# Masked graph attention on one core: the exchanged products move one step later, the squares come early, and each exchange row becomes one run

## The chip, the cores and the metric

The kernel runs on one core of a Trainium2 chip. The metric is the device time of a whole run in microseconds. A core has TensorE (matrix products; in the profile PE, its weight loads PEld), VectorE (DVE), ScalarE (ACT), GpSimd (POOL) and SyncE (SP), which here only issues transfers. Each engine works through its own queue in order. Semaphores order the engines among one another.

## The reference, cut to what matters

```python
# M = N = 6144, D = 128, TEMPERATURE = 0.07
h = jnp.maximum(_layernorm(x), 0.0)
scores = jnp.where(adj > 0, jnp.einsum('md,de,ne->mn', h, weight, nodes), -2**32 + 1)
out = x + jax.nn.softmax(scores / TEMPERATURE, axis=1) @ nodes
```

`adj` is int32, 6144 x 6144, with about one entry in 1,500 set. It is 151 MB, and all of it has to be read.

## The kernel before

The output is made in 48 tiles of 128 rows. For one tile `u` there are these stages, all of which run over its 6144 columns:

- **h**: layer norm of x (statistics on VectorE, `make_h` on GpSimd), split into two fp16 halves (`split_h`), and turned by a transposing DMA (`hT`).
- **scores**: TensorE, six chunks of 1024 columns, six matmuls each, into the two PSUM tiles `ps_s`. Chunk j can start when chunk j-2 has been masked.
- **mask**: VectorE (L603), six chunks: score less code, and the row's maximum. The codes are the adjacency, which is loaded in three chunks of 2048 columns (`load_adj`, 1 MB each, SyncE) and turned into codes by GpSimd (`convert`, L425). The buffer `adj_i` holds one tile, so chunk c of the next tile is loaded when both masks over chunk c are done. `find_max` (L611, L613) ends the row's maximum.
- **exp**: ScalarE, one piece of 2048 columns (`exp_p`, L491) and four pieces of 1024 (`exp_e`, L497).
- **turning**: the products need the probabilities transposed. The first 2048 columns are turned on TensorE (`turn`, L813, four turns of 512 columns into the three PSUM banks `ps_t`) and split into fp16 halves by ScalarE (`hi_p`, L522) and VectorE (`lo_p`, L618). The other 4096 columns are turned as 32 x 32 squares on VectorE (`turn_squares`, L630, four pieces) and then exchanged between the four groups of 32 partitions by 16 SBUF to SBUF transfers of 128 KB (`exchange`, L338, SyncE). ScalarE (`hi_e`, L505, four pieces) and GpSimd (`lo_e`, L444, eight turns) split them.
- **product**: TensorE adds twelve turns into `ps_o`: `product_p` 0 to 3 for the turned ones, `product_e` 0 to 7 for the exchanged ones. `finish` (VectorE) scales and adds x, and ScalarE stores.

The tiles are worked on in a pipeline written out by hand. In step t, scores and masks belong to tile t+2, exp and squares to tile t+1, turns and products to tile t (`product_e` 4 to 7 to tile t-1), and `make_h` to tile t+3. Steps 3 to 38 are a hardware loop of six iterations with six steps in each; the steps before and after are written out.

The order of SyncE's queue in a step is: adjacency chunk 2 of t+2, x of t+4, adjacency chunk 0 of t+3, the transpose of h, eight exchange transfers of t+1, adjacency chunk 1 of t+3, eight exchange transfers, x for the residual. ScalarE's order is: `exp_e` 0 to 2, `hi_p` 0 and 1, the store, `exp_e` 3, `hi_e` 0, `hi_p` 2 and 3, `hi_e` 1 to 3, `exp_p`. VectorE's is: mask 0, square 0, mask 1, `finish`, square 1, `lo_p` 0 and 1, mask 2, square 2, `lo_p` 2 and 3, mask 3, square 3, mask 4, the sum, statistics, mask 5, `find_max`. GpSimd's is: `lo_e` 6 and 7 of t-1, convert chunk 1, `make_h`, `split_h`, convert chunk 2, `lo_e` 0 to 5, convert chunk 0.

`hi_e` waits for all 16 transfers of its tile:

```python
act.wait_ge(exchanged[s], exchanges(u, s))
```

Of the kernel before, what the change touches and what calls it, by code (L numbers as in the profile page):

```python
# [5 lines left out]
def gnn_masked_attention_kernel(  # L6
# [71 lines left out]
    EARLY_E = 4  # L78
# [19 lines left out]
    with ctx:  # L98
# [15 lines left out]
        pT_hi = sb("pT_hi", [P, BANKS, TURN], fp16)  # L114
        pT_lo = sb("pT_lo", [P, BANKS, TURN], fp16)
# [3 lines left out]
        h_centred = sb("h_centred", [P, 2, D], fp32)  # L119
# [4 lines left out]
        fin_a = sb("fin_a", [P, 2, D], fp32)  # L124
# [15 lines left out]
        nodes_max = sb("nodes_max", [P, 1], fp32)  # L140
        nodes_top = sb("nodes_top", [P, 1], fp32)
# [6 lines left out]
        w_sum = sb("w_sum", [P, 1], fp32)  # L148
        w_top = sb("w_top", [P, 1], fp32)
        y_bound = sb("y_bound", [P, 1], fp32)  # L150
# [112 lines left out]
        def exchanged_part(r, c):  # L263


            return probs[:, r, columns(E_FIRST + E_PART * c, E_PART)].rearrange("q (a k i) -> q a k i", a=QUADS, i=QUAD)
# [36 lines left out]
        def _(sp):  # L303
# [54 lines left out]

# [20 lines left out]
        def _(pool):  # L379
# [7 lines left out]
            def make_h(u, s):  # L387
                pool.wait_ge(aggr_done, u + 1)
# [8 lines left out]
                nc.gpsimd.tensor_scalar(h_centred[:, s, :], x_ln[:, s, :], mean_var[:, s, 0:1], 0.0,  # L397
# [6 lines left out]
                nc.gpsimd.tensor_scalar(h[:, s, :], h_centred[:, s, :], rstd[:, s, :], 1.0, ALU.mult, ALU.mult)\  # L404
# [72 lines left out]
            for m in range(E_TURNS - E_PART, E_TURNS):  # L477
# [3 lines left out]
        def _(act):  # L481
# [478 lines left out]
```

## Time and profile before

| | |
|---|---|
| median of 3 runs | 1142.36 us (1138.94 to 1143.82) |
| profiled execution | 1133.46 us, span 1131.7 us |
| mean granted clock of TensorE | 0.97 |
| TensorE busy (modelled) | 82% of the span |
| GpSimd busy | 75% |
| VectorE busy | 70% |
| ScalarE busy | 58% |
| SyncE's DMA queue | 264 MB, 82% of 16 engines |

The span runs from the first to the last instruction of the profiled execution. Busy shares are means over a span whose stages overlap; idle time of an engine matters only where it delays the work that sets the end. Matmuls are pipelined and their ends are modelled, so the busy time of TensorE counts overlaps. The releaser behind an idle time is inferred from semaphores. An instruction row of the timeline gives its start, its length, engine, line, operation, output and input; "x2" means that two have been merged.

### The profile page before, as it was taken

Reading aid. Unit: us, or ns where it says so; the run is one execution under the profiler, and the core shown is the slowest. Engines: PE = TensorE matmul, PEld = TensorE weight load, DVE = VectorE, ACT = ScalarE, POOL = GpSimd, SP = SyncE. Lnnn points to the kernel's source line nnn. Section 1 sums busy time; section 2 is a strip of 40 time slices with the busy share of each in tenths; the row PEclk is TensorE's granted clock in tenths of the full one; section 3 lists DMA queues with packets and bytes.
Section 4 is the critical chain, followed back from the end, with each engine's and each line's share of the span. In section 5 each row is a group of like instructions: output and inputs, shape, how many; then the busy total and the mean of one; then the engine's idle time right before and its main releaser. Section 6 shows DMA issues by size and latency. Waiting matters only on the chain.

```text
span 1131.7 us, 23242 instructions
## 1 busy us (share of the span) xinstructions
PE 930.1 (82%) x7182; PEld 614.6 (54%) x7182; DVE 790.5 (70%) x1430; ACT 652.5 (58%) x896; POOL 844.2 (75%) x825
## 2 busy tenths in 40 slices
PE   7688888879788797896978878888789888888876
PEld 4255555556555465563655545555556555555555
DVE  6777677767676676775776657767676776777672
ACT  5466555655565555654565545646565665656563
POOL 4967887786778767787678776778678778878755
PEclk9999999999999998999999989999999999999999
DMA  9489889887988879889788887889978988998873
GB/s 317 150 212 280 225 250 265 250 246 213 246 270 228 250 208 269 237 255 240 200 267 232 253 254 202 238 235 262 267 211 242 266 275 228 260 282 228 221 185 83
DMA packets 171522, 268.81 MB, mean 238 GB/s; under 512 B 29968, under 2 KB 152976, under 8 KB 152976
## 3 DMA queue, kind: packets, MB, share of 16 engines
q1 hardware_dynamic: 164208, 264.05, 82.0%
q10 hardware_dynamic: 7200, 3.28, 1.4%
q8 instruction: 67, 1.10, 0.4%
q14 instruction: 47, 0.39, 0.1%
HBM read 160.50 MB, written 3.15 MB: 145 GB/s over the span
## 4 chain that ended last, share of the span: by engine, by line
SPq 24%; PE 16%; issue 14%; DMA 13%; DVE 12%; POOL 8%; ACT 7%; ACTq 1%; DVEq 1%; POOLq 0%
SPq L338 22%; PE ps_s L795 7%; POOL nodes_raw L444 7%; DMA probs<-nodes_raw 5%; PE ps_o L822 5%; DMA probs<-squares_own 5%; ACT pT_e_hi L505 4%; DVE probs L603 4%; DMA adj_i<-in_adj_dram 3%; ACT pT_hi L522 3%; DVE pT_lo L618 2%; PE ps_o L825 2%; DVE nodes_raw L630 2%; DVE squares_own L630 2%; PE ps_t L813 2%
## 5 line engine op out<-in xcount | busy, mean ns | idle before, releaser
L603 DVE CUSTOM_DVE_ANT_0 probs<-ps_s,adj_i 128x1024 f32<-128x1024 f32 x282 | 343.0, 1217 | 242.3 <-POOL adj_i L425 104.0
L444 POOL TENSOR_TENSOR nodes_raw<-probs,pT_e_hi 128x512 f16<-128x512 f32 x384 | 433.4, 1163 | 19.6 <-ACT pT_e_hi L505 19.6
L795 PE MATMUL ps_s<-yT_hi,hT 128*128 128x512 f16 x1152 | 402.0, 391 | 36.5 <-issue 26.2
L425 POOL TENSOR_SCALAR adj_i<-adj_i 128x2048 uint32<-128x2048 int32 x141 | 268.6, 1905 | 214.5 <-DMA adj_i<-in_adj_dram 208.9
L497 ACT ACTIVATE probs<-probs,neg_max,exp_scale 128x1024 f32<-128x1024 f32 x192 | 237.1, 1236 | 197.3 <-DVE neg_max L613 191.2
L822 PE MATMUL ps_o<-v,pT_e_hi 128*128 128x256 f16 x1536 | 287.8, 277 | 50.2 <-POOL nodes_raw L444 47.2
L825 PE MATMUL ps_o<-v,nodes_raw 128*128 128x128 f16 x1536 | 271.6, 221 | 0.0
L505 ACT ACTIVATE pT_e_hi<-probs 128x1024 f16<-128x1024 f32 x192 | 192.4, 1057 | 113.7 <-DMA probs<-squares_own 65.3
L822 PE MATMUL ps_o<-v,pT_hi 128*128 128x256 f16 x768 | 145.5, 283 | 103.8 <-DVE pT_lo L618 103.7
L795 PE MATMUL ps_s<-yT_lo,hT 128*128 128x512 f16 x576 | 225.7, 392 | 0.0
L822 PEld LDWEIGHTS ps_o<-v,pT_e_hi 128*128 128x128 f16 x1536 | 151.8, 99 | 129.1 <-POOL nodes_raw L444 98.6
L795 PEld LDWEIGHTS ps_s<-yT_hi,hT 128*128 128x128 f16 x1152 | 115.5, 100 | 155.5 <-issue 48.1
L522 ACT ACTIVATE pT_hi<-ps_t 128x512 f16<-128x512 f32 x192 | 103.5, 591 | 134.9 <-PE ps_t L813 134.8
L822 PEld LDWEIGHTS ps_o<-v,pT_hi 128*128 128x128 f16 x768 | 77.2, 101 | 158.1 <-DVE pT_lo L618 132.6
L825 PEld LDWEIGHTS ps_o<-v,nodes_raw 128*128 128x128 f16 x1536 | 152.0, 99 | 15.3 <-issue 2.2
L618 DVE TENSOR_TENSOR pT_lo<-ps_t,pT_hi 128x512 f16<-128x512 f32 x192 | 121.7, 674 | 47.6 <-ACT pT_hi L522 47.6
L825 PE MATMUL ps_o<-v,pT_lo 128*128 128x128 f16 x768 | 139.5, 226 | 0.0
L630 DVE STREAM_TRANSPOSE nodes_raw<-probs 128x1024 f32<-128x1024 f32 x96 | 119.0, 1239 | 1.4 <-ACT probs L497 1.4
L630 DVE STREAM_TRANSPOSE squares_own<-probs 128x1024 f32<-128x1024 f32 x96 | 119.0, 1239 | 0.5 <-ACT probs L497 0.5
L491 ACT ACTIVATE probs<-probs,neg_max,exp_scale 128x2048 f32<-128x2048 f32 x48 | 100.4, 2092 | 8.6 <-DVE neg_max L613 8.6
L813 PE MATMUL ps_t<-ident,probs 128*128 128x128 f32 x768 | 100.3, 274 | 0.0
L813 PEld LDWEIGHTS ps_t<-ident,probs 128*128 128x128 f32 x768 | 82.7, 141 | 1.5 <-issue 0.3
(72 smaller groups left out, 537.8 us busy)
## 6 DMA issues: line engine op xcount, KB each, us to landing
adj_i<-in_adj_dram SPq DMA_DIRECT2D x141, 1024.0 KB, 6.5
probs<-squares_own SPq DMA_DIRECT2D x384, 128.0 KB, 3.1
probs<-nodes_raw SPq DMA_DIRECT2D x384, 128.0 KB, 3.6
nodes_raw<-in_L_gnn_input_dram SPq DMA_DIRECT2D x6, 512.0 KB, 7.0
x_res<-in_x_dram SPq DMA_DIRECT2D x48, 64.0 KB, 4.5
probs<-in_adj_dram SPq DMA_DIRECT2D x3, 1024.0 KB, 14.1
out_dram<-fin ACTq DMA_DIRECT2D x48, 64.0 KB, 4.8
x_ln<-in_x_dram SPq DMA_DIRECT2D x46, 64.0 KB, 5.8
```

What stands on the lines that cost most here:

```text
L338: sp.dma_start(to.rearrange("j (c a x) -> j c a x", a=QUADS, c=E_PARTS)[:, :, a, :], squares[s][a * QUAD:(a + 1) * QUAD, b, :, :].rearrang ...
L425: nc.gpsimd.tensor_scalar(codes(u, c), adjacency(u, c), PRESENT_STEP, ABSENT, ALU.mult, ALU.add)\
L444: nc.gpsimd.tensor_tensor(lo, exchanged_part(r, c)[:, :, g * PER_TURN:(g + 1) * PER_TURN, :], hi, ALU.subtract)\
L497: nc.scalar.activation(part, part, ACT.Exp, bias=neg_max[:, s, :], scale=exp_scale[:, :], accum_out=chunk_sum[:, s, 1 + c:2 + c]).then_inc ...
L505: nc.scalar.activation(e_halves(pT_e[0], E_PART * c, E_PART), exchanged_part(r, c), ACT.Copy)\
L603: nc.vector.tensor_tensor_reduce(out=probs[:, r, j * SCORE:(j + 1) * SCORE], in0=ps_s[j % 2][:, :], in1=codes(u, c)[:, part * SCORE:(part ...
L618: nc.vector.tensor_tensor(pT_lo[:, P_BANK[q], :], ps_t[P_BANK[q]][:, :], pT_hi[:, P_BANK[q], :], ALU.subtract)\
L630: nc.vector.transpose(squares[s][:, :, c * blocks:(c + 1) * blocks, :], of).then_inc(squared, 1)
L795: made = nc.tensor.matmul(ps_s[j % 2][:, q * 512:(q + 1) * 512], hT[:, s, part, :], y[:, cols], start=(part == 0 and y is yT_hi), stop=(pa ...
L813: made = nc.tensor.transpose(ps_t[P_BANK[q]][:, b * P:(b + 1) * P], probs[:, r, q * TURN + b * P:q * TURN + (b + 1) * P], ident[:, :])
L822: nc.tensor.matmul(ps_o[:, 0:2 * D], hi[b], v[:, blk, :, :].rearrange("p s d -> p (s d)"), start=(order == 0 and b == 0), stop=(order == T ...
L825: made = nc.tensor.matmul(ps_o[:, 0:D], lo[b], v[:, blk, 0, :], start=False, stop=(order == TURNS - 1 and b == PER_TURN - 1), skip_group_c ...
```

## The change

- TensorE takes all eight `product_e` of tile t-1 in step t, between the score chunks 0 to 3; then `product_p` 0 and 1 after chunk 4 and 2 and 3 after chunk 5.
- `pT_hi` and `pT_lo` have four buffers of one turn each, where there were three. `hi_p` waits for the product of the step before from its own buffer alone.
- ScalarE does all four `exp_e`, then `hi_p` 0 and 1, four `hi_e`, `hi_p` 2 and 3, the store and `exp_p`.
- VectorE does the squares 1 to 3 right after mask 1, and `finish` after mask 3.
- In the exchange, a piece of a row lies in one run of 4 KB in source and target, where there were four runs of 1 KB. The exchanged pieces of a turn are therefore spread over all 4096 columns, and masks 2 to 5 of a tile wait for all eight `lo_e` of the tile that was in the buffer.
- GpSimd does three `lo_e` of t-1, then `make_h` and `split_h`, convert chunk 1, three `lo_e`, convert chunk 2, two `lo_e`, convert chunk 0.
- `h_centred` has one buffer (`make_h` waits for `h_done`), `fin_a` is gone (`finish` writes `fin` twice), and some scalars share one tensor.
- SyncE's order stays.

```diff
-    EARLY_E = 4
+    LATE_LO = 3
...
-        pT_hi = sb("pT_hi", [P, BANKS, TURN], fp16)
-        pT_lo = sb("pT_lo", [P, BANKS, TURN], fp16)
+        pT_hi = sb("pT_hi", [P, P_TURNS, TURN], fp16)
+        pT_lo = sb("pT_lo", [P, P_TURNS, TURN], fp16)
...
-            return probs[:, r, columns(E_FIRST + E_PART * c, E_PART)].rearrange("q (a k i) -> q a k i", a=QUADS, i=QUAD)
+            all_of_it = probs[:, r, columns(E_FIRST, E_TURNS)].rearrange("q (a k i) -> q a k i", a=QUADS, i=QUAD)
+            return all_of_it[:, :, E_PART * PER_TURN * c:E_PART * PER_TURN * (c + 1), :]
...
-                        sp.dma_start(to.rearrange("j (c a x) -> j c a x", a=QUADS, c=E_PARTS)[:, :, a, :],
-                                     squares[s][a * QUAD:(a + 1) * QUAD, b, :, :].rearrange("j (c k) i -> j c (k i)", c=E_PARTS))\
+                        sp.dma_start(to.rearrange("j (a x) -> j a x", a=QUADS)[:, a, :],
+                                     squares[s][a * QUAD:(a + 1) * QUAD, b, :, :].rearrange("j k i -> j (k i)"))\
...
             def make_h(u, s):
+                if not (isinstance(u, int) and u == 0):
+                    pool.wait_ge(h_done, u)
...
                 if at != 0:
-                    for m in range(E_TURNS - E_PART, E_TURNS):
+                    for m in range(E_TURNS - LATE_LO, E_TURNS):
                         lo_e(t - 1, (r - 1) % PROBS, m)
-                if has(at, 2):
-                    convert(t + 2, 1)
                 if has(at, 3):
                     make_h(t + 3, 1 - par)
                     split_h(t + 3, 1 - par)
                 if has(at, 2):
+                    convert(t + 2, 1)
+                for m in range(0, 3):
+                    lo_e(t, r, m)
+                if has(at, 2):
                     convert(t + 2, 2)
-                for m in range(E_TURNS - E_PART):
+                for m in range(3, E_TURNS - LATE_LO):
                     lo_e(t, r, m)
...
             def hi_p(t, q, at):
                 act.wait_ge(turned, t * P_TURNS + (q + 1))
-                if P_BANK.index(P_BANK[q]) != q:
-
-                    act.wait_ge(pv_done, t * TURNS + (P_BANK.index(P_BANK[q]) + 1))
-                elif at != 0:
-                    act.wait_ge(pv_done, t * TURNS + (max(k for k in range(P_TURNS) if P_BANK[k] == P_BANK[q]) + 1 - TURNS))
-                nc.scalar.activation(pT_hi[:, P_BANK[q], :], ps_t[P_BANK[q]][:, :], ACT.Copy).then_inc(hi_done, 1)
+                if at != 0:
+
+                    act.wait_ge(pv_done, t * TURNS + (q + 1 - TURNS))
+                nc.scalar.activation(pT_hi[:, q, :], ps_t[P_BANK[q]][:, :], ACT.Copy).then_inc(hi_done, 1)
...
                 if has(at, 1):
-                    for c in range(3):
+                    for c in range(E_PARTS):
                         exp_e(t + 1, nxt, n, c)
                 for q in range(2):
+                    hi_p(t, q, at)
+                for c in range(E_PARTS):
+                    hi_e(t, par, r, c, at)
+                for q in range(2, P_TURNS):
                     hi_p(t, q, at)
...
-                if has(at, 1):
-                    exp_e(t + 1, nxt, n, 3)
-                hi_e(t, par, r, 0, at)
-                for q in range(2, P_TURNS):
-                    hi_p(t, q, at)
-                for c in range(1, E_PARTS):
-                    hi_e(t, par, r, c, at)
...
-                    dve.wait_ge(lo_e_done, (u - PROBS) * E_TURNS + E_PART * (j - 1))
+                    dve.wait_ge(lo_e_done, (u - PROBS) * E_TURNS + E_TURNS)
...
                 next_mask(0)
                 next_squares(0)
                 next_mask(1)
+                for c in range(1, E_PARTS):
+                    next_squares(c)
+                next_mask(2)
+                lo_p(t, 0)
+                lo_p(t, 1)
+                next_mask(3)
                 if at != 0:
                     finish(t - 1, nxt, at is None or at > 2)
-                next_squares(1)
-                lo_p(t, 0)
-                lo_p(t, 1)
-                next_mask(2)
-                next_squares(2)
                 lo_p(t, 2)
                 lo_p(t, 3)
-                next_mask(3)
-                next_squares(3)
                 next_mask(4)
...
-                for j in range(2):
-                    scores(t, par, j, at)
+                def last_products(m, turns):
                     if at != 0:
-                        for m in range(EARLY_E + 2 * j, EARLY_E + 2 * j + 2):
-                            product_e(t - 1, m, None if at is None else at - 1)
-                for j in range(2, 4):
-                    for q in range(2 * j - 4, 2 * j - 2):
-                        turn(t, r, q, at)
-                    scores(t, par, j, at)
-                    if j == 2 and at != 0:
-                        pe.wait_ge(fin_done, t)
-                    for q in range(2 * j - 4, 2 * j - 2):
-                        product_p(t, q, at)
-                for j in range(4, SCORES):
-                    scores(t, par, j, at)
-                    for m in range(2 * j - 8, 2 * j - 6):
-                        product_e(t, m, at)
+                        for k in range(m, m + turns):
+                            product_e(t - 1, k, None if at is None else at - 1)
+
+                scores(t, par, 0, at)
+                last_products(0, 2)
+                scores(t, par, 1, at)
+                last_products(2, 2)
+                for q in range(2):
+                    turn(t, r, q, at)
+                scores(t, par, 2, at)
+                last_products(4, 2)
+                scores(t, par, 3, at)
+                last_products(6, 2)
+                for q in range(2, P_TURNS):
+                    turn(t, r, q, at)
+                scores(t, par, 4, at)
+                if at != 0:
+                    pe.wait_ge(fin_done, t)
+                for q in range(2):
+                    product_p(t, q, at)
+                scores(t, par, 5, at)
+                for q in range(2, P_TURNS):
+                    product_p(t, q, at)
```

## Rows read from the trace of the kernel before

**Rows 1.** The page: busy time of the engines, and the queue of SyncE.

```profile
PE 930.1 (82%) x7182; PEld 614.6 (54%) x7182; DVE 790.5 (70%) x1430; ACT 652.5 (58%) x896; POOL 844.2 (75%) x825
...
q1 hardware_dynamic: 164208, 264.05, 82.0%
```

**Rows 2.** Line 611, which ends a step: its 48 instructions, first and last.

```profile
L611 DVE TENSOR_REDUCE row_max<-chunk_max x48: 158/159/160, 42.0 to 1093.7; 128x1 f32<-128x6 f32 x48
```

**Rows 3.** Six steps in one window: busy us, clock, DMA share, GB/s.

```profile
core 0: us, PE busy (x) PEld busy (x) DVE busy (x) ACT busy (x) POOL busy (x), PEclk, DMA share, GB/s
874.40:1004.20 129.80, 110.96 (x890) 73.41 (x888) 96.12 (x174) 78.96 (x108) 103.48 (x103) 1.00 0.90 256
```

**Rows 4.** Waits of those six steps: total us, times, longest.

```profile
ACT probs L497 <- DVE neg_max L613: 25.1, 6, 4.4
...
POOL adj_i L425 <- DMA adj_i<-in_adj_dram: 15.6, 9, 2.8
DVE probs L603 <- POOL adj_i L425: 15.4, 7, 2.6
```

**Rows 5.** Timeline of ScalarE, then of VectorE, around one landing.

```profile
925.44 1.24 ACT L497 ACTIVATE probs<-probs,neg_max,exp_scale 128x1024 f32<-128x1024 f32 x1
...
928.62 1.06 ACT L505 ACTIVATE pT_e_hi<-probs 128x1024 f16<-128x1024 f32 x1 [1.84 <-DMA probs<-squares_own]
929.59 1.07 ACT L522 ACTIVATE pT_hi<-ps_t 128x512 f16<-128x512 f32 x2
930.54 2.96 ACT L505 ACTIVATE pT_e_hi<-probs 128x1024 f16<-128x1024 f32 x3
933.38 2.10 ACT L491 ACTIVATE probs<-probs,neg_max,exp_scale 128x2048 f32<-128x2048 f32 x1
...
930.20 1.29 DVE L618 TENSOR_TENSOR pT_lo<-ps_t,pT_hi 128x512 f16<-128x512 f32 x2 [0.68 <-ACT pT_hi L522]
931.40 1.22 DVE L603 CUSTOM_DVE_ANT_0 probs<-ps_s,adj_i 128x1024 f32<-128x1024 f32 x1
932.54 1.24 DVE L630 STREAM_TRANSPOSE nodes_raw<-probs 128x1024 f32<-128x1024 f32 x1
```

**Rows 6.** Timeline of SyncE's queue: exchange issues.

```profile
912.54 5.16 SPq L338 DMA_DIRECT2D probs<-squares_own  x8
...
918.39 5.97 SPq L338 DMA_DIRECT2D probs<-squares_own  x8
...
933.87 5.18 SPq L338 DMA_DIRECT2D probs<-nodes_raw  x8
```

**Rows 7.** Timeline of TensorE where the loop goes back.

```profile
528.93 0.39 PE L795 MATMUL ps_s<-yT_hi,hT 128*128 128x512 f16 x1 [2.99 <-issue]
...
535.88 0.61 PE L795 MATMUL ps_s<-yT_hi,hT 128*128 128x512 f16 x1 [4.17 <-issue]
```

**Rows 8.** Timeline of GpSimd in one step.

```profile
926.05 0.19 POOL L390 TENSOR_SCALAR var_eps<-mean_var 128x1 f32<-128x1 f32 x1
...
929.08 0.43 POOL L416 TENSOR_TENSOR h_split<-h,h_split 128x128 f16<-128x128 f32 x1
931.37 1.93 POOL L425 TENSOR_SCALAR adj_i<-adj_i 128x2048 uint32<-128x2048 int32 x1 [1.86 <-DMA adj_i<-in_adj_dram]
933.26 6.76 POOL L444 TENSOR_TENSOR nodes_raw<-probs,pT_e_hi 128x512 f16<-128x512 f32 x6
```

**Rows 9.** Issues of lines 338 and 309: ns min/median/max.

```profile
L338 SPq DMA_DIRECT2D probs<-squares_own x384: 585/607/1932, 54.1 to 1098.0; - x192
...
L309 SPq DMA_DIRECT2D adj_i<-in_adj_dram x141: 327/365/1927, 10.4 to 1079.3; - x141
```

**Rows 10.** Windows: exchange alone, exchange with a backlog, adjacency.

```profile
1107.00:1116.00 9.00, 6.90 (x72) 5.52 (x70) 1.90 (x4) 2.35 (x4) 4.21 (x4) 1.00 0.90 207
...
923.00:926.00 3.00, 2.76 (x22) 1.74 (x19) 2.96 (x7) 1.65 (x3) 1.91 (x1) 1.00 1.13 229
927.00:932.00 5.00, 4.39 (x42) 3.28 (x40) 4.32 (x7) 3.38 (x5) 2.46 (x5) 1.00 1.06 404
```

**Rows 11.** Timeline of VectorE near the end.

```profile
1104.10 1.24 DVE L630 STREAM_TRANSPOSE nodes_raw<-probs 128x1024 f32<-128x1024 f32 x1
```

More of the change, by code:

```diff
@@ L118, in gnn_masked_attention_kernel @@
         hT = sb("hT", [P, 2, 2, P], fp16)
-        h_centred = sb("h_centred", [P, 2, D], fp32)
+        h_centred = sb("h_centred", [P, D], fp32)
         h = sb("h", [P, 2, D], fp32)
@@ L123, in gnn_masked_attention_kernel @@
         x_res = sb("x_res", [P, 2, D], fp32)
-        fin_a = sb("fin_a", [P, 2, D], fp32)
         fin = sb("fin", [P, 2, D], fp32)
@@ L139, in gnn_masked_attention_kernel @@
         part_max = sb("part_max", [P, NODE_PARTS], fp32)
-        nodes_max = sb("nodes_max", [P, 1], fp32)
-        nodes_top = sb("nodes_top", [P, 1], fp32)
+        head_scalars = sb("head_scalars", [P, 5], fp32)
+        nodes_max, nodes_top, w_sum, w_top, y_bound = [head_scalars[:, i:i + 1] for i in range(5)]
         field = sb("field", [P, 1], int32)
@@ L396, in make_h @@
                 pool.sem_inc(pool_waited, 1)
-                nc.gpsimd.tensor_scalar(h_centred[:, s, :], x_ln[:, s, :], mean_var[:, s, 0:1], 0.0,
+                nc.gpsimd.tensor_scalar(h_centred[:, :], x_ln[:, s, :], mean_var[:, s, 0:1], 0.0,
                                         ALU.subtract, ALU.max).then_inc(h_centred_done, 1)
@@ L403, in make_h @@
                 pool.sem_inc(pool_waited, 1)
-                nc.gpsimd.tensor_scalar(h[:, s, :], h_centred[:, s, :], rstd[:, s, :], 1.0, ALU.mult, ALU.mult)\
+                nc.gpsimd.tensor_scalar(h[:, s, :], h_centred[:, :], rstd[:, s, :], 1.0, ALU.mult, ALU.mult)\
                     .then_inc(h_done, 1)
@@ L476, in _ @@
             steps(pool, step)
-            for m in range(E_TURNS - E_PART, E_TURNS):
+            for m in range(E_TURNS - LATE_LO, E_TURNS):
                 lo_e(LAST, LAST % PROBS, m)
@@ L617, in lo_p @@
                 dve.wait_ge(hi_done, split_count(t, q))
-                nc.vector.tensor_tensor(pT_lo[:, P_BANK[q], :], ps_t[P_BANK[q]][:, :], pT_hi[:, P_BANK[q], :], ALU.subtract)\
+                nc.vector.tensor_tensor(pT_lo[:, q, :], ps_t[P_BANK[q]][:, :], pT_hi[:, q, :], ALU.subtract)\
                     .then_inc(split_freed, 1)
@@ L644, in finish @@
                 dve.wait_ge(x_res_in[s], loads(u, s))
+                if free:
+                    dve.wait_ge(stored[s], loads(u - 2, s))
                 dve.wait_ge(pv_done, u * TURNS + TURNS)
-                nc.vector.scalar_tensor_tensor(out=fin_a[:, s, :], in0=ps_o[:, 0:D], scalar=inv_sum[:, s, :],
+                nc.vector.scalar_tensor_tensor(out=fin[:, s, :], in0=ps_o[:, 0:D], scalar=inv_sum[:, s, :],
                                                in1=x_res[:, s, :], op0=ALU.mult, op1=ALU.add)\
@@ L649, in finish @@
                 dve.wait_ge(fin_a_done, u + 1)
-                if free:
-                    dve.wait_ge(stored[s], loads(u - 2, s))
                 nc.vector.scalar_tensor_tensor(out=fin[:, s, :], in0=ps_o[:, D:2 * D], scalar=inv_sum[:, s, :],
-                                               in1=fin_a[:, s, :], op0=ALU.mult, op1=ALU.add)\
+                                               in1=fin[:, s, :], op0=ALU.mult, op1=ALU.add)\
                     .then_inc(fin_done, 1)
@@ L831, in product_p @@
                 pe.wait_ge(split_freed, split_count(t, q))
-                multiply(q, [pT_hi[:, P_BANK[q], b * P:(b + 1) * P] for b in range(PER_TURN)],
-                         [pT_lo[:, P_BANK[q], b * P:(b + 1) * P] for b in range(PER_TURN)], q, at)
+                multiply(q, [pT_hi[:, q, b * P:(b + 1) * P] for b in range(PER_TURN)],
+                         [pT_lo[:, q, b * P:(b + 1) * P] for b in range(PER_TURN)], q, at)
             def product_e(t, m, at):
@@ L915, in step @@
             def step(t, par, r, at):
[L916 to L917 removed]
+                def last_products(m, turns):
                     if at != 0:
[L919 to L932 removed]
+                        for k in range(m, m + turns):
[20 more added lines that the diff above has]
+                    product_p(t, q, at)
             steps(pe, step)
[L935 removed]
+            for m in range(E_TURNS):
                 product_e(LAST, m, LAST)
```

4 lines of the change are left out of this document (removed).

## Prediction, made before the change was run

> **What bounds the kernel now.** I began with the page's busy line and queue line [rows 1]. No engine is near full: TensorE 82%, GpSimd 75%, VectorE 70%, ScalarE 58%; but the 16 DMA engines spend 82% of the span on SyncE's queue. A bound is then either the DMA stream or a loop through several queues. The mark of a step is `find_max`: 48 of them lie between 42.0 and 1093.7 us [rows 2], so a step takes 22.4 us on average. For a stretch without disturbance I took the six steps from 874.4 to 1004.2 us: 21.6 us each, with VectorE busy 16.0, ScalarE 13.2, GpSimd 17.2, TensorE 18.5 (modelled) and the DMA share 0.90, so 19.5 us of DMA [rows 3]. Two to five microseconds of every step belong to no engine. The waits of that stretch say where: ScalarE for the maximum, GpSimd for adjacency landings, VectorE for GpSimd's codes [rows 4]. These point round in a circle, so I followed one event in the timeline. ScalarE starts `hi_e` 0 at 928.62, the moment the exchange has landed; behind it on the same in-order engine stand `hi_p` 2 and 3 (929.59); then VectorE does `lo_p` 2 and 3 (930.20), mask 3 (931.40) and square 3 (932.54), and only now may SyncE start the next exchange, at 933.87 [rows 5]. That is 5.25 us from landing to issue. The exchange before it was issued from 912.54 and had landed at 928.62: 16.1 us. 5.25 + 16.1 = 21.3 us is the step. The 16.1 are 8 issues in 5.2, an adjacency issue between, 8 more issues in 6.0 [rows 6], and the rest landing behind the 1 MB of adjacency in the same queue. So the bound is a one-step loop: an exchange cannot begin until the exchange before it has landed, because the last square stands behind work that waits for that landing.
>
> A second loss comes every six steps, when the loop goes back: TensorE waits for "issue" twice, 2.99 and 4.17 us [rows 7]. It and other irregularities are the 0.75 us by which the mean step (22.4) exceeds the quiet one.
>
> **The change part by part.**
>
> *Squares early.* All four squares of t+1 now stand behind masks 0 and 1 alone. ScalarE does the four `exp_e` first. Let T be the start of mask 0. Masks take 1.15 to 1.2 us from start to start, squares 1.16 (932.54 less 931.40 is 1.14) [rows 5], so two masks and four squares end near T+7.2; `exp_e` 3 is done about T+4.6, since `exp_e` starts before mask 0. No work is added, it is the same 16.0 us of VectorE. The loop of rows 5 is cut: squares no longer wait for `lo_p` 2 and 3.
>
> *Products one step later.* TensorE takes the eight exchanged products of t-1 in step t, between scores 0 to 3. `hi_e`(t) moves behind four `exp_e` and `hi_p` 0 and 1. An exchange whose squares end at T+7.2 lands, by the 16.1 us above, at T+23.3. With a step P of 19.2 this is 4.1 us into the next step; `hi_e` comes up there at about 6 us (four `exp_e` at 1.24, two `hi_p` at 0.54 [rows 5]). Slack about 2 us, so the wait for the landing goes. What is late next is the loop over two steps: landing, four `hi_e`, two `hi_p`, `exp_p`, four `exp_e`, a square, an exchange: 3.9 + 1.1 + 2.1 + 4.9 + 1.2 + 16.1 = 29.3 us for two steps, 14.7 for one. It does not bind.
>
> *Waits added.* Masks 2 to 5 wait for all eight `lo_e` of t-1. GpSimd does its last three first in its step, 3.4 us, and mask 2 stands at T+7.2: covered. Without that cover lo_p, masks and finish queue behind it and TensorE waits for them. The wait on `h_done` names GpSimd's own earlier result: nothing. Convert 1 moves behind `make_h` and `split_h`: three `lo_e` 3.4, `make_h` and split 3.5 (926.05 to 929.51), convert 1.9: it ends at T+8.8, and mask 2 waits up to 1.6 us for it; masks 3 to 5 queue behind. TensorE has eight products, two score chunks and turns in that time, so scores 4 is where it shows. I leave 1.6 of VectorE per step: 16.0 + 1.6 + about 0.6 of handshakes = 18.2.
>
> *Four half buffers, one `fin`, one `h_centred`.* `hi_p` 3 no longer waits for product 0 of its tile; bank 0 of `ps_t` is still shared, so turn 3 still waits for `lo_p` 0. The second `finish` operation reads the row the first wrote, as before. Nothing either way; the operations are of the same shape.
>
> *Adjacency and queue order.* SyncE issues the same 16 exchange DMAs, three adjacency loads, two x loads and a transpose in the same order. The adjacency load amid the exchange waits for mask 3, which now comes after the squares (about T+11.5); the first 8 issues run until about T+13, so it is covered, and if issues get cheaper the DMA queue has a backlog to live on.
>
> *The exchange's shape.* Each row of an exchange DMA is now one run of 4 KB instead of four of 1 KB. The trace shows no such transfer. Issue costs 0.61 us at four runs a row, and at best 0.33, the shortest adjacency issue [rows 9]; I take 0.5, and it is off the path once the transfers themselves are the slower. The transfer: with nothing else moving, the exchange shows 0.90 share at 207 GB/s, so 230 GB/s at full share; with a backlog 229; adjacency moves at 404 [rows 10]. If 4 KB runs go as 1 KB runs, 16 take 2.1 MB / 229 = 9.2 us; if they reach the adjacency's rate, 5.2. A bad end is not excluded: each of the 16 engines gets two runs in place of eight, less to overlap. I take twice the time as a worst case, 18.3. Nearest is the same source, target and engines, so I take 9.2, hardly changed.
>
> The rate alone fits the row above. The Trainium skill, "DMA: Bandwidth & Descriptors", section "Why small descriptors are slow (HBM only)", holds that SBUF to SBUF transfers don't suffer from small descriptors, and puts the fixed price at about 3 cycles on each packet's 32-byte beats. As an estimate from that page, 35 beats for 1 KB against 131 for 4 KB is 6% less, so the exchange would be 8.6 us in place of 9.2. No row of the trace before can show it.
>
> **The new step.** GpSimd: eight `lo_e` at 1.12 (six in 6.76), three converts at 1.9, `make_h` and split 3.5 [rows 8] = 18.2. DMA: 9.2 + 3.15 MB / 404 = 7.8, + 1 to 1.5 for x, the output and the transpose = 18.0 to 18.5, and at the share of now at most 19.5. TensorE at most 18.5, VectorE 18.2. Four resources within half a microsecond: the floor is 18.3, and they won't all fit without gaps. I take 19.2, between the floor and 19.5 of DMA with a few tenths of gaps. The gain is 21.6 - 19.2 = 2.4 us on 46 steps, 110 us. The 0.75 us of irregularity I keep: TensorE has no room to catch up 7 us.
>
> The tail: the last square starts at 1104.10 and ends at 1105.3 now [rows 11], behind turns and low halves; with `exp_e` of the last tile from 1094.1 they would end about 1100.3. The exchange, the eight `lo_e` and the products then follow as before: about 4 us. In the start the products come later and the scores do not: nothing.
>
> Span 1131.7 - 110 - 4 = 1018. The profiled execution took 1133.46, 1.8 more than its span, so 1020; the median of the runs, 1142.36, is 0.8% above the profiled one, so **1028 us**.
>
> **The rivals.** A: the 4 KB runs are cheap. At 5.2 us an exchange the DMA stream falls to 14.5 and only the compute floors are left; a step of 18.4, another 0.8 x 46 = 37 us: 990. For it: adjacency, in 8 KB runs, goes at 404. Against: the exchange at 230 with nothing beside it, where packets have no rival to wait for.
>
> B: the gaps. GpSimd and VectorE wait for each other twice a step (convert to mask, `lo_e` to product to `finish`), and a full DMA queue lands adjacency late; if the 15.6 us of waits for it in six steps [rows 4] stay, they and GpSimd's 18.2 make 20.8, with a little overlap 20.5: 1028 + 1.3 x 46 = 1088.
>
> C: nothing gained. The exchange was never the only reason: the step is 21 to 22 because the DMA stream (19.5 us by its share) with its pauses is. 1120 to 1150. Against it: the 5.25 us of [rows 5], in which the next exchange waits for nothing but the last square.
>
> D, slower: the 4 KB runs are slow. `hi_e` blocks ScalarE in order, with `hi_p` 2 and 3 and `exp_p` behind it. With the rest of DMA at 9.1 us, the step exceeds today's 21.6 once an exchange DMA takes over 0.78 us against 0.57 now. At twice the time the step is 18.3 + 9.1 = 27.4 us: 1142 + 5.8 x 46 = 1409, and at 0.9 us each 23.5: 1230.
>
> **Numbers.** Forecast 52% (1000 to 1055), A 18%, B 20%, C 4%, D 6%. The range leaves out C and D, and a quarter of A and of B, whose own spreads reach past the ends: 985 to 1095. A change of 0.5% is about what a measurement of this kernel can tell. Faster 0.91, same 0.02, slower 0.07.
>
> **What would show it.** Right: `hi_e` no longer waits for exchanged data; the last square to the first exchange issue lies near T+7; steps near 19.2; DMA share 0.93 or more; GpSimd above 90% within a step. The exchange alone near 207 to 230 GB/s says the shape did nothing, near 400 says A. Wrong: steps over 20.5 with waits of VectorE for `adj_i`, or of ScalarE for landings. The forecast falls if a wait I count as covered (mask 2 for convert 1, TensorE for `finish`, SyncE for mask 3) grows beyond 2 us.

## The result and the profile after

The changed kernel takes 1008.35 us (median of 4 runs, 1006.03 to 1012.51) beside 1142.01 us for the kernel before; the ratio is 0.884, 95% interval 0.880 to 0.887. Predicted were 1028 us in a range of 985 to 1095. The same kernel run again beside three experiments gave 1009.19 us and 0.887 (0.880 to 0.894). The kernel before varied between groups of runs (medians 1131 to 1142), so experiments are compared by their ratio to the kernel before on the same chip.

The page of the changed kernel, first the busy line and SyncE's queue, then line 606, which ends a step as 611 did:

```profile
PE 890.9 (88%) x7182; PEld 618.5 (61%) x7182; DVE 791.6 (79%) x1430; ACT 646.6 (64%) x896; POOL 842.6 (84%) x825
...
q1 hardware_dynamic: 90480, 264.05, 95.6%
```

```profile
L606 DVE TENSOR_REDUCE row_max<-chunk_max x48: 158/159/160, 39.8 to 972.5; 128x1 f32<-128x6 f32 x48
```

VectorE, ScalarE and GpSimd are busy as long as in [rows 1] to within 1%, and TensorE does the same 7182 matmuls (its modelled busy time is 39 us less); the same work lies in a shorter span, and the DMA queue has gone from 82 to 95.6%. The span fell by 1131.7 - 1007.0 = 124.7 us. Of these, 2.2 lie ahead of the first mark (42.0 against 39.8) and 3.5 behind the last (38.0 against 34.5); 119.0 are steps: 47 of them took 1051.7 us [rows 2] and take 932.7. A step fell from 22.4 to 19.85 us. Six quiet ones, in the view of [rows 3]:

```profile
857.40:972.50 115.10, 107.07 (x901) 75.89 (x899) 95.74 (x170) 77.78 (x108) 100.00 (x97) 1.00 1.03 282
```

That is 19.2 us a step, the number of the forecast (the mean of the 37 steps that remain from the sixth mark on, without the long step of every six, is 19.35), with a DMA share of 1.03 (transfers overlap a little, so it can pass 1) and 282 GB/s against 256. The waits, for the whole span:

```profile
POOL nodes_raw L442 <- ACT pT_e_hi L505: 98.3, 45, 6.9
DVE probs L598 <- POOL adj_i L423: 75.9, 67, 1.9
...
ACT pT_e_hi L505 <- DMA probs<-squares_own: 50.1, 20, 4.2
...
ACT pT_e_hi L505 <- DMA probs<-nodes_raw: 42.8, 18, 4.0
```

Here is the first thing that I had not forecast: `hi_e` still waits for exchanged data, 92.9 us in 38 steps. The timelines of SyncE, ScalarE and GpSimd over one step show why, in the manner of [rows 5, 6]:

```profile
788.77 5.43 SPq L335 DMA_DIRECT2D probs<-nodes_raw  x8
794.47 0.40 SPq L306 DMA_DIRECT2D adj_i<-in_adj_dram  x1
794.92 5.77 SPq L335 DMA_DIRECT2D probs<-nodes_raw  x8
...
788.72 3.90 ACT L505 ACTIVATE pT_e_hi<-probs 128x1024 f16<-128x1024 f32 x4 [2.03 <-DMA probs<-squares_own]
...
807.79 3.90 ACT L505 ACTIVATE pT_e_hi<-probs 128x1024 f16<-128x1024 f32 x4 [2.17 <-DMA probs<-nodes_raw]
...
789.96 3.39 POOL L442 TENSOR_TENSOR nodes_raw<-probs,pT_e_hi 128x512 f16<-128x512 f32 x3 [0.82 <-ACT pT_e_hi L505]
```

The exchange issued from 788.77 has landed at 807.79: 19.0 us, where it took 16.1. SyncE issues as fast as before; the transfers stand in a queue that is now always full. It is not this exchange alone: the median from issue to landing of one transfer, in the kernel before and then in the changed one, is

```profile
probs<-squares_own SPq DMA_DIRECT2D x384, 128.0 KB, 3.1
probs<-nodes_raw SPq DMA_DIRECT2D x384, 128.0 KB, 3.6
```

```profile
probs<-squares_own SPq DMA_DIRECT2D x384, 128.0 KB, 6.6
probs<-nodes_raw SPq DMA_DIRECT2D x384, 128.0 KB, 7.5
```

The chain of waits over two steps names a loop again:

```profile
780.35 3.39 POOL nodes_raw L442 x3
...
787.36 1.21 SPq L359
...
799.34 8.35 DMA probs<-nodes_raw
...
811.26 1.17 POOL nodes_raw L442
...
818.36 2.29 POOL nodes_raw L442 x2
```

From `lo_e` at 780.35 it goes over `make_h`, `split_h` and the transpose of h, behind which the exchange stands in SyncE's queue, to the landing at 807.69, to `hi_e`, and through GpSimd's codes and halves to 818.36: 38.0 us, two steps of 19.0. So the exchange is in a loop still, but in one that spans two steps and has most of GpSimd's work in it. It is not the only loop of this length. From 641.50 to 681.07, 39.6 us, the chain runs from GpSimd over mask 2, `finish`, TensorE's products and `hi_e` back to GpSimd without any landing. The page puts 14% of the chain on the exchange's issues and 10% on its landings, against 22 and 10% before.

### The profile page after: what moved, and what is told of

Read it like the earlier page. It is cut to its first block, busy times and chain, and to the rows that moved or that the text cites. A ratio compares the mean times of both kernels' runs of the same rounds, so it can differ in the third digit from the quotient of the medians.

```text
span 1007.0 us, 23278 instructions
## 1 busy us (share of the span) xinstructions
PE 890.9 (88%) x7182; PEld 618.5 (61%) x7182; DVE 791.6 (79%) x1430; ACT 646.6 (64%) x896; POOL 842.6 (84%) x825
## 3 DMA queue, kind: packets, MB, share of 16 engines
q1 hardware_dynamic: 90480, 264.05, 95.6%
## 4 chain that ended last, share of the span: by engine, by line
PE 24%; POOL 21%; SPq 16%; issue 14%; DMA 10%; DVE 6%; ACT 4%; POOLq 0%; DVEq 0%; ACTq 0%
SPq L335 14%; POOL nodes_raw L442 12%; PE ps_s L789 10%; PE ps_o L816 8%; DMA probs<-nodes_raw 6%; POOL adj_i L423 5%; DMA probs<-squares_own 4%; PE ps_o L819 4%; ACT pT_e_hi L505 3%; DVE probs L598 2%; PE ps_t L807 2%; DVE pT_lo L613 1%; POOL h_centred L395 1%; SPq L359 1%; POOL rstd L391 1%
## 5 line engine op out<-in xcount | busy, mean ns | idle before, releaser
L598 DVE CUSTOM_DVE_ANT_0 probs<-ps_s,adj_i 128x1024 f32<-128x1024 f32 x282 | 343.3, 1218 | 147.9 <-POOL adj_i L423 75.9
L789 PE MATMUL ps_s<-yT_hi,hT 128*128 128x512 f16 x1152 | 396.7, 386 | 45.6 <-issue 29.9
L816 PE MATMUL ps_o<-v,pT_e_hi 128*128 128x256 f16 x1536 | 276.8, 275 | 0.0
L423 POOL TENSOR_SCALAR adj_i<-adj_i 128x2048 uint32<-128x2048 int32 x141 | 268.3, 1903 | 10.2 <-DMA adj_i<-in_adj_dram 10.0
L819 PE MATMUL ps_o<-v,nodes_raw 128*128 128x128 f16 x1536 | 266.3, 220 | 0.0
L505 ACT ACTIVATE pT_e_hi<-probs 128x1024 f16<-128x1024 f32 x192 | 188.4, 1046 | 112.2 <-DMA probs<-squares_own 50.1
L789 PE MATMUL ps_s<-yT_lo,hT 128*128 128x512 f16 x576 | 222.6, 386 | 0.0
L816 PE MATMUL ps_o<-v,pT_hi 128*128 128x256 f16 x768 | 138.6, 274 | 19.2 <-DVE fin L647 14.6
L807 PE MATMUL ps_t<-ident,probs 128*128 128x128 f32 x768 | 108.0, 276 | 40.5 <-DVE pT_lo L613 40.5
L819 PE MATMUL ps_o<-v,pT_lo 128*128 128x128 f16 x768 | 132.7, 220 | 0.0
L625 DVE STREAM_TRANSPOSE nodes_raw<-probs 128x1024 f32<-128x1024 f32 x96 | 113.9, 1223 | 3.1 <-ACT probs L497 1.4
L625 DVE STREAM_TRANSPOSE squares_own<-probs 128x1024 f32<-128x1024 f32 x96 | 113.9, 1223 | 2.3 <-ACT probs L497 0.6
L816 PEld LDWEIGHTS ps_o<-v,pT_hi 128*128 128x128 f16 x768 | 75.5, 98 | 52.4 <-DVE fin L647 33.1
## 6 DMA issues: line engine op xcount, KB each, us to landing
probs<-in_adj_dram SPq DMA_DIRECT2D x3, 1024.0 KB, 14.5
```

The costliest lines, as they stand in the source:

```text
L423: nc.gpsimd.tensor_scalar(codes(u, c), adjacency(u, c), PRESENT_STEP, ABSENT, ALU.mult, ALU.add)\
L505: nc.scalar.activation(e_halves(pT_e[0], E_PART * c, E_PART), exchanged_part(r, c), ACT.Copy)\
L598: nc.vector.tensor_tensor_reduce(out=probs[:, r, j * SCORE:(j + 1) * SCORE], in0=ps_s[j % 2][:, :], in1=codes(u, c)[:, part * SCORE:(part ...
L625: nc.vector.transpose(squares[s][:, :, c * blocks:(c + 1) * blocks, :], of).then_inc(squared, 1)
L789: made = nc.tensor.matmul(ps_s[j % 2][:, q * 512:(q + 1) * 512], hT[:, s, part, :], y[:, cols], start=(part == 0 and y is yT_hi), stop=(pa ...
L807: made = nc.tensor.transpose(ps_t[P_BANK[q]][:, b * P:(b + 1) * P], probs[:, r, q * TURN + b * P:q * TURN + (b + 1) * P], ident[:, :])
```

## The experiments

**1. `hi_p` 2 and 3 ahead of `hi_e` 0, in the kernel before.** It tests the loop that the prediction named as the bound.

```diff
-                hi_e(t, par, r, 0, at)
                 for q in range(2, P_TURNS):
                     hi_p(t, q, at)
-                for c in range(1, E_PARTS):
+                for c in range(E_PARTS):
```

> The kernel before with one edit: ScalarE does hi_p 2 and 3 ahead of hi_e 0. Theory (the 21.3 us step is the one-step loop landing, hi_e 0, hi_p 2 and 3, lo_p, mask 3, square 3, next exchange): the loop is cut, a quiet step falls to 19.5 to 20.5 us and the time to 1035 to 1085 us. Rival (a second loop of nearly the same length stands behind it: landing, hi_e, eight lo_e on GpSimd, the last products, finish, square 1, and the squares behind it, over two steps): the step stays at 21 to 21.6 and the time within 1.5% of 1142 us.

1117.04 us, 0.986 (0.978 to 0.995). That is outside the theory's 1035 to 1085 us and within the rival's 1.5%. The marks of its steps, in VectorE's timeline:

```profile
883.42 0.16 DVE L610 TENSOR_REDUCE row_max<-chunk_max 128x1 f32<-128x6 f32 x1
901.43 0.16 DVE L610 TENSOR_REDUCE row_max<-chunk_max 128x1 f32<-128x6 f32 x1
924.97 0.16 DVE L610 TENSOR_REDUCE row_max<-chunk_max 128x1 f32<-128x6 f32 x1
945.49 0.16 DVE L610 TENSOR_REDUCE row_max<-chunk_max 128x1 f32<-128x6 f32 x1
968.84 0.16 DVE L610 TENSOR_REDUCE row_max<-chunk_max 128x1 f32<-128x6 f32 x1
```

Steps of 18.0, 23.5, 20.5 and 23.4 us: single steps can now be short, but a pair still takes 41.5 and 43.9. The loop of one step was real: the waits of `hi_e` for landings fell from 110.8 to 17.6 us in the whole run. What stands behind it here is not the exchange loop that the rival named, though. Pieces of this kernel's chain, over one step:

```profile
886.61 6.70 DMA adj_i<-in_adj_dram
...
893.51 1.91 POOL adj_i L425
...
902.93 7.05 DMA adj_i<-in_adj_dram
...
910.16 1.91 POOL adj_i L425
...
917.50 1.17 DVE nodes_raw L629
```

The exchange is issued from 897.48, the adjacency chunk stands behind eight of its transfers in SyncE's queue and lands at 909.98, GpSimd makes codes of it, then come masks, `lo_p` 2 and 3, mask 3 and square 3, and the next exchange is issued at 918.75: 21.3 us, one step. This loop goes through an adjacency landing. On the page of this run 9% of the chain are adjacency landings and 1% exchange landings; in the kernel before it was 3% and 10%. In other stretches, as from 949 to 986, the chain goes round over GpSimd's halves, the products, `finish` and `hi_e` without a landing.

In the kernel before there is a loop of two steps as well, of nearly the length of two short ones. It can be followed there: `hi_e` 0 after a landing at 907.29, `lo_e` from 911.83, the last of them done at 922.7, `finish` at 924.15, then the squares behind it, and the exchange from 933.87, landed at 950.85: 43.6 us for two steps.

**2. Squares early alone, in the kernel before.** The products stay where they were.

```diff
-                    for c in range(3):
+                    for c in range(E_PARTS):
                         exp_e(t + 1, nxt, n, c)
...
                 next_mask(1)
+                for c in range(1, E_PARTS):
+                    next_squares(c)
                 if at != 0:
                     finish(t - 1, nxt, at is None or at > 2)
-                next_squares(1)
```

> The kernel before with the squares 1 to 3 right after mask 1 and exp_e 3 with the others, ahead of finish; the products stay in their step, the exchange keeps four runs a row. Theory (early squares are what cuts every loop through the exchange): 1010 to 1060 us, most of the gain. Rival (the products have to move too, since mask 5 and find_max wait behind products that wait for lo_e): 1080 to 1130 us.

1083.4 us, 0.955 (0.949 to 0.962): two fifths of the whole gain, as the rival said, but not for the reason it gave. TensorE and VectorE at one place of a step:

```profile
716.50 0.28 PE L819 MATMUL ps_o<-v,pT_hi 128*128 128x256 f16 x1 [2.61 <-DVE pT_lo L616]
...
711.74 3.49 DVE L628 STREAM_TRANSPOSE nodes_raw<-probs 128x1024 f32<-128x1024 f32 x3
...
715.76 1.28 DVE L616 TENSOR_TENSOR pT_lo<-ps_t,pT_hi 128x512 f16<-128x512 f32 x2
```

TensorE stands still for 2.6 us, because `product_p` 0 comes right after scores 2, and its low half stands behind three squares. Of the 47 steps 19 take 20.22 to 20.24 us and none after the first is shorter. What holds them there is a loop of TensorE and VectorE alone, without the exchange; on the page 56% of the chain are TensorE's and 2% landings. The waits of TensorE's products for `lo_p` are 133.6 us in this run and 4.6 in the changed kernel (there its turns wait 40.5 for `lo_p`). This is what moving the products does: products that need nothing from this step fill the hole that early squares tear into TensorE's step. The changed kernel differs from this one in GpSimd's order, the four half buffers and the order of `lo_p` and `finish` too; these were not tried one by one.

**3. Squares late, in the changed kernel.** The complement: products late, squares 2 and 3 behind `lo_p` 1 and mask 3.

```diff
-                for c in range(1, E_PARTS):
-                    next_squares(c)
+                next_squares(1)
                 next_mask(2)
                 lo_p(t, 0)
                 lo_p(t, 1)
+                next_squares(2)
                 next_mask(3)
+                next_squares(3)
```

> The changed kernel with VectorE's squares late again: square 1 after mask 1, square 2 after lo_p 1, square 3 after mask 3. Theory (the exchange has to start early in the step to land before hi_e needs it): the last square ends some 5 us later, hi_e and GpSimd wait for the landing, a quiet step of 20 to 20.8 us, the time 1045 to 1090 us. Rival (products one step later leave slack enough, squares early are not needed): 1005 to 1020 us.

1084.95 us, 0.956 (0.950 to 0.962), in the theory's range. The steps are longer than its 20 to 20.8, 21.3 us at the mean of the 37 without the sixth ones; the sixth is 22.5 where the changed kernel's is 25.2. The waits:

```profile
ACT probs L497 <- DVE neg_max L608: 156.0, 47, 4.0
POOL nodes_raw L442 <- ACT pT_e_hi L505: 149.4, 48, 7.2
...
PE ps_o L817 <- DVE fin L647: 102.6, 46, 2.8
...
ACT pT_e_hi L505 <- DMA probs<-squares_own: 64.0, 16, 5.0
```

Both waits that the theory names are there (the landing 135 us with the other buffer's, against 92.9 in the changed kernel, GpSimd for `hi_e` 149 against 98), and TensorE waits another 103 for `finish` (14.6 in the changed kernel), since squares 2 and 3 now stand between mask 2, which waits for codes, and `finish`. How much of the loss is the late landing and how much the late `finish` is not taken apart. Early squares alone are worth 4.5%, all the rest of the change without them 4.4%, both together 11.5%.

**4. The shape of the exchange,** in both kernels: 4 KB runs put into the kernel before, and 1 KB runs back into the changed one.

```diff
-                        sp.dma_start(to.rearrange("j (c a x) -> j c a x", a=QUADS, c=E_PARTS)[:, :, a, :],
-                                     squares[s][a * QUAD:(a + 1) * QUAD, b, :, :].rearrange("j (c k) i -> j c (k i)", c=E_PARTS))\
+                        sp.dma_start(to.rearrange("j (a x) -> j a x", a=QUADS)[:, a, :],
+                                     squares[s][a * QUAD:(a + 1) * QUAD, b, :, :].rearrange("j k i -> j (k i)"))\
```

> The kernel before with one run of 4 KB in each row of the exchange, and masks 2 to 5 waiting for all eight lo_e. Theory (the shape does little, the transfer is as slow as with four runs of 1 KB): 1125 to 1150 us. Rival (bigger runs make the exchange faster, and the landing comes earlier in the loop): 1085 to 1120 us.

> The changed kernel with the exchange's four runs of 1 KB a row, all else as changed. Theory (the shape does little): 1000 to 1020 us. Rival (with the DMA queues full, per-run work and 0.1 us more at each issue count): 1025 to 1060 us.

The kernel before with 4 KB: 1129.34 us, 0.997 (0.993 to 1.001), no change. Its packet records give 286 ns for a run of 4 KB at the median; in the kernel before one of 1 KB took 72, and four of them 288. The changed kernel with 1 KB: 1016.02 us, 0.898 (0.891 to 0.904) against 0.884 (0.880 to 0.887) and 0.887 (0.880 to 0.894) of the changed kernel: about 1% slower, but the second interval touches, so it is not settled. The queue is full there, and all exchange packets together took 524 us of the 16 engines against 489, 7% more. In the kernel before it was 438 against 418, 5%. The Trainium skill, "DMA: Bandwidth & Descriptors", section "Why small descriptors are slow (HBM only)", holds that SBUF to SBUF transfers don't suffer from small descriptors; in packet time they do here, by 5 and 7%, near the 6% that the prediction worked out as an estimate from the section's price per packet.

The four sums also part shape and queue. Per step they are 9.1 us (1 KB, queue with pauses), 8.7 (4 KB, with pauses), 10.9 (1 KB, full) and 10.2 (4 KB, full): the longer runs take a little off, and the full queue adds 1.5 us and more.

**5. What bounds the changed kernel.** Three cuts, each of which leaves work out. Half of each exchange transfer left out:

```diff
-                        sp.dma_start(to.rearrange("j (a x) -> j a x", a=QUADS)[:, a, :],
-                                     squares[s][a * QUAD:(a + 1) * QUAD, b, :, :].rearrange("j k i -> j (k i)"))\
+                        sp.dma_start(to.rearrange("j (a x) -> j a x", a=QUADS)[:, a, 0:TURN],
+                                     squares[s][a * QUAD:(a + 1) * QUAD, b, 0:TURN // QUAD, :].rearrange("j k i -> j (k i)"))\
```

> The changed kernel with half of the exchange left out: each of the 16 transfers moves 2 KB of its 4 KB a row, so the output isn't the reference's. DMA work falls by some 4.5 us a step, everything else is as it was. Theory (a quiet step of 19.0 us is set by a loop through the exchange, full DMA queues and GpSimd): the waits of hi_e for landings go and the step falls to GpSimd's 18.2 to 18.4 us, the time to 970 to 985 us. Rival (engines alone set it, the landing waits cost nothing): 1000 to 1012 us.

Half of GpSimd's codes left out:

```diff
-                nc.gpsimd.tensor_scalar(codes(u, c), adjacency(u, c), PRESENT_STEP, ABSENT, ALU.mult, ALU.add)\
+                nc.gpsimd.tensor_scalar(codes(u, c)[:, 0:SCORE], adjacency(u, c)[:, 0:SCORE], PRESENT_STEP, ABSENT, ALU.mult, ALU.add)\
```

> The changed kernel with half of GpSimd's codes left out (each convert takes 1024 of its 2048 columns), so the output isn't the reference's. GpSimd's work falls by 2.9 us a step. Theory (the loop runs through GpSimd as well as through the exchange; DMA share is 1.04, so the stream can't follow far): the step falls by 0.2 to 0.8 us, 970 to 1000 us. Rival (GpSimd alone is the bound): the step falls by 1 us or more to TensorE's 17.7 to 18, 945 to 965 us. Second rival (DMA alone is the bound): no change.

Both:

> Both cuts at once, half of the exchange and half of the codes left out. Theory: with the stream and GpSimd out of the way TensorE and the handshakes between it and VectorE are left, a step of 17.7 to 18.2 us, 940 to 965 us. Rival (the step's order on VectorE and TensorE already binds at 18.5 or more): 975 to 990 us, no better than one cut alone.

And the unedited kernel beside them:

> The changed kernel unedited, so that the three runs beside it and those of the call before have it on their own chip. Expected 0.88 to 0.89 of the kernel before.

| | us | ratio (interval) | mean of the 37 steps, us |
|---|---|---|---|
| changed kernel | 1009.19 | 0.887 (0.880 to 0.894) | 19.35 |
| half the exchange | 958.19 | 0.842 (0.836 to 0.849) | 18.03 |
| half the codes | 997.02 | 0.878 (0.871 to 0.884) | 19.15 |
| both | 923.62 | 0.810 (0.803 to 0.818) | 17.44 |

The half exchange and both together came out below their ranges (970 to 985, 940 to 965), half the codes within its own.

Windows of the three cut kernels, in this order, four, four and three quiet steps:

```profile
739.60:812.00 72.40, 70.68 (x593) 50.22 (x592) 64.00 (x117) 52.12 (x72) 68.60 (x68) 1.00 0.84 248
```

```profile
745.30:820.90 75.60, 72.34 (x604) 50.60 (x603) 64.39 (x117) 51.63 (x72) 58.47 (x69) 1.00 1.04 288
```

```profile
711.40:763.70 52.30, 52.30 (x446) 37.92 (x444) 47.87 (x88) 39.15 (x54) 43.89 (x52) 1.00 0.87 250
```

With half the exchange, GpSimd is busy 68.6 of 72.4 us and waits for nothing in this window but its own results in `make_h`, so it is full: 18.1 us, the prediction's 18.2. The waits of `hi_e` for landings are down from 92.9 to 7.2 us. With half the codes GpSimd has 17 us of slack in four steps, but the DMA share stays at 1.04 and the step hardly moves: four such steps of the changed kernel take 75.5 us, these 75.6. The waits of `hi_e` for landings grow from 92.9 to 123.8 us instead. So a shorter GpSimd part of the loop buys little while the queue is full; whether the stream by itself or the loop through it sets the step, these runs do not tell apart. With both, TensorE is busy for all of the 52.3 us, and each step takes 17.45. So the order of the bounds is the stream with its loop (19.2 to 19.35), GpSimd (18.1), TensorE (17.45). I had put GpSimd and the stream level.

**6. No jump back.** All 48 steps written out.

```diff
-            with eng.Fori(HEAD, TILES - TAIL, UNROLL) as i:
-                for k in range(HEAD, HEAD + UNROLL):
-                    step(i + (k - HEAD) if k > HEAD else i, k % 2, k % PROBS, None)
-            for t in range(TILES - TAIL, TILES):
+            for t in range(HEAD, TILES):
```

> The changed kernel with all 48 steps written out, so that nothing jumps back. Theory (the long step of every six, 25 us where the others take 19 to 20, comes from the jump back and the instructions that have to be fetched behind it): those steps go, five of them at 5 to 6 us each, 975 to 985 us. Rival (instructions stream in at the same cost with or without the jump): 1000 to 1015 us, stalls spread.

986.45 us, 0.868 (0.862 to 0.874), 1.5 us over the theory's range. In the changed kernel every sixth step takes about 25 us, and TensorE waits in it as in [rows 7], now once and longer:

```profile
722.97 0.61 PE L789 MATMUL ps_s<-yT_hi,hT 128*128 128x512 f16 x1 [5.68 <-issue]
```

There are five such waits, 29.9 us in all. They cost more than themselves, because TensorE's clock falls in them. Two windows, the wait and what follows it:

```profile
717.90:722.90 5.00, 0.00 (x0) 0.00 (x0) 0.39 (x4) 4.50 (x7) 4.62 (x7) 0.65 1.05 323
722.90:730.00 7.10, 7.03 (x46) 4.40 (x47) 3.57 (x6) 0.50 (x2) 3.26 (x5) 0.77 0.95 252
```

TensorE does nothing in the first, and the granted clock falls to its lower level, 1.2 GHz, until 726.2: a score matmul takes 0.63 us there and 0.38 behind it, and the first chunk with its products is some 1.5 us longer than one at 2.4 GHz. Written out, the granted clock stays at 2.4 GHz from 68 to 959 us, no step is longer than 20.7 once the pipeline is full, and this kind of wait is down to 9.9 us in 21 small ones of the weight loads. But the 37 other steps are 19.55 us at the mean instead of 19.35, and `hi_e` waits 123.9 us for landings instead of 92.9: of the 29 us that the five long steps were over the others, the run got back 20. That the loop costs the time is shown; its jump and its counted semaphore values went together, and what TensorE's sequencer does there is not shown.

**7. Another order of the exchange.** Neighbouring transfers alternate between the lower and the upper 64 partitions, in source and in target.

```diff
-                for a in quads:
-                    for b in range(QUADS):
+                pairs = [(g + 2 * h, (k + 2 * h) % QUADS) for g in range(quads[0] // 2, (quads[-1] + 1) // 2)
+                         for k in range(QUADS) for h in range(2)]
+                for a, b in pairs:
```

> The changed kernel with the 16 exchange transfers in another order: neighbours in the queue read from and write to groups of 32 partitions from different halves of the 128. Theory (a 4 KB packet takes 302 ns at the median and 168 at the tenth percentile because neighbours press on the same part of SBUF's 128 partitions): the median packet falls under 250 ns, the DMA share of a quiet step under 1.0, and the quiet step towards the 18.1 us that half an exchange gave, 965 to 990 us. Rival (the order has no effect, an exchange packet takes what it takes within one transfer): 1004 to 1014 us.

993.93 us, 0.876 (0.870 to 0.882), 1.2% under the changed kernel, with intervals that touch, and between the two ranges. Experiments 6 and 8, which differ in this order alone, settle that it has an effect: 0.868 (0.862 to 0.874) against 0.856 (0.850 to 0.861), 1.5%. The mechanism as I had put it fell: the median packet went from 302 to 287 ns only, and the share did not fall. The same four steps of the changed kernel and of this one:

```profile
761.00:836.60 75.60, 70.77 (x591) 49.79 (x589) 64.40 (x119) 52.08 (x72) 68.89 (x69) 1.00 1.04 287
```

```profile
743.94:817.97 74.03, 70.87 (x591) 49.92 (x590) 64.29 (x117) 52.21 (x72) 68.97 (x69) 1.00 1.04 292
```

They take 18.5 us each at 292 GB/s, against 18.9 at 287; over the 37 steps it is 18.88 against 19.35. The stream moves 2% more in the same time. Whether partitions press on one another in another way, or whether it is the time at which single transfers land, is open.

**8. Both of these.**

> Both at once, the other order of the exchange and all 48 steps written out. Theory: the two gains add up, 935 to 965 us. Rival (without effect of either): within the better of the two alone.

971.75 us, 0.856 (0.850 to 0.861). From 1009.2 the two alone gave 22.7 and 15.3 us; together they give 37.4, so they add up. The range, 935 to 965, had counted on more from the order. This is the fastest kernel of the study with the full computation, 14.5% under the kernel before.

## Why the prediction was right

*The bound of the kernel before.* A loop through the exchange, not an engine: right (experiments 1 to 3). But "the bound is a one-step loop" was a part of it: experiment 1 cuts just this loop and brings 1.4%. A loop of two steps through `lo_e`, the products and `finish`, and one of a step through an adjacency landing, are as long. The change helps since early squares stand in none of the three: they wait for no exchange landing, for no adjacency chunk but the first, and for no `lo_p` and no `finish` of their step. The waits of GpSimd for adjacency, which rival B let stay, fell from 208.9 us to 96.8 in experiment 2 and 10.0 in the changed kernel.

*What the products do.* The prediction saw in them only slack for the landing. The runs show a second, larger reason: without them early squares leave TensorE waiting for `lo_p`, and the step stops at 20.23. The number came out all the same, because I had built the new step from the load of each engine, and this assumes that the order leaves no such hole.

*The wait for the landing.* "Slack about 2 us, so the wait for the landing goes" failed. Counted from the start of mask 0, T, `hi_e` came up at T+5.9 as forecast, but the data landed at T+8 and not at T+4.1. I had carried over the 16.1 us of an exchange in a queue with pauses; in the full queue it is 19.0. The first issue is at T+7.9 (788.77 less 780.83) and not T+7.2, since it stands behind the transpose of h in SyncE's queue (787.36, 1.21 us). The wait stayed at 92.9 us of 110.8, 2 us a step; half an exchange takes it away and brings 1.3 us a step. The prediction's loop of two steps had ScalarE in it (29.3 us) and not GpSimd.

*Waits added.* Mask 2 for convert 1: "up to 1.6 us"; at 789.87 it is 1.90, and all waits of masks for codes are 75.9 us, 1.6 a step (104.0 in the kernel before). The wait of masks 2 to 5 for `lo_e` isn't among the waits, covered as foreseen. TensorE waits for `finish` about 0.3 us a step.

*The exchange's shape.* "Hardly changed" held: with 4 KB runs the exchange in the kernel before took 8.7 us of the engines a step, with 1 KB 9.1; 9.2 was forecast, with 8.6 as an estimate beside it. With nothing else in the queue it moved 221 GB/s at a share of 0.94 (982 to 985 us), in the range of 207 to 230 that was to say so. The full queue made it 10.2. An issue costs 0.59 us at the median, where 0.5 was taken. Rivals A and D fell with it, and A's step was about right: with half an exchange it is 18.1 (A said 18.4), though the time is then 958 and not 990 us.

*The step.* 19.2 forecast, 19.2 measured in six steps and 19.35 over 37; floor of GpSimd 18.2 against 18.1 measured. That it came so near is in part luck. 19.2 was not worked out from a loop but taken between the floor and the 19.5 of DMA, for gaps; the wait for the landing had been put at nothing, and the DMA sum of 18.0 to 18.5 was too small: a share of 1.03 over 19.2 us is 19.8. Its rates in [rows 10] were read unevenly: 207 GB/s was scaled up to a full share, but 229 at a share of 1.13 and 404 at 1.06 were not scaled down. Scaled, they are 203 and 381 GB/s, and the sum is 10.3 + 8.3 + 1 to 1.5, so 19.6 to 20.1 us. GpSimd is busy 87% of these steps, where over 90 was to show that the forecast was right. Rivals B and C fell: waits for adjacency are 10.0 us in the whole run.

*The sum.* 1020 us were forecast for the profiled execution and 1008.8 came. Of the 11 us, 9 are steps (119 gained, not 110: irregular parts shrank from 0.75 to 0.65 us a step, and there are 47 intervals, not 46), 2.2 are the start, which I had put at nothing. The other 8 us of 1028 came from scaling by the median of before, which stood 0.8% over its profiled execution; that of the changed kernel does not.

## What to carry to other kernels

Where no engine is full and a step is steady, follow one landing through every in-order queue back to the next issue, and then look for a second loop over two steps before pricing the cut of the first: cutting one of three loops of nearly the same length brought 1.4%, early squares, which cut them all, 4.5%. After each cut read the chain again: it can run through a transfer that was not in the picture, here the adjacency that queues behind the exchange. Work that is moved early on one engine opens a hole on the engine that waits behind it, and something that needs nothing from this step has to fill it; early squares alone were worth 4.5%, the rest alone 4.4%, both 11.5%. When a stretch gets shorter, transfer latencies don't stay: the same exchange took 16.1 us in a queue with pauses and 19.0 in a full one.

## What the hardware did that I had not expected

A jump back cost TensorE a wait of about 6 us in the changed kernel and two waits of 3 and 4 us in the one before, and the granted clock fell to 1.2 GHz in the wait and stayed there for some 3 us of work behind it; a program with all steps written out ran 2% faster. A packet of 4 KB between SBUF partitions took 302 ns at the median and 168 at the tenth percentile, where one of 8 KB from HBM took 315, and one of 2 KB, with half the exchange left out, 121. The order of the 16 transfers alone, with the same bytes and shapes, brought 1.5% of the time and moved the stream from 287 to 292 GB/s in the same four steps. One exchange transfer took 3.1 to 3.6 us from issue to landing at the median in the queue with pauses and 6.6 to 7.5 in the full one.
